# The order of work in the first, the twenty-second and the last tile of a quantized convolution and feed-forward kernel

## The chip, the cores and the metric

The kernel runs on one NeuronCore of one Trainium2 chip. Its engines are TensorE (PE, whose weight loads are listed as PEld), VectorE (DVE), ScalarE (ACT), GpSimd (POOL) and SyncE (SP, which issues nearly all DMAs; its queue is called SPq). They run side by side and wait for one another on semaphores. The metric is the device time of one execution in microseconds (us). Before the change the median of three runs is 294.35 us (294.17 to 295.05).

## The reference

For x of shape (128, 32, 512), the work is a grouped one-dimensional convolution with a per-sample shift, then a feed-forward block in which every activation and every weight is rounded to 8-bit steps of its row, and the residual:

```python
out = conv_general_dilated(x, weight, padding=[(4, 4)], feature_group_count=4)   # 32 -> 32 channels, 9 taps
out = out + ctx[:, :, None] + bias[None, :, None]

def fake_quant(t, axis):
    s = jnp.max(jnp.abs(t), axis=axis, keepdims=True) / 127.0
    s = jnp.maximum(s, 1e-08)
    return jnp.clip(jnp.round(t / s), -128.0, 127.0) * s     # (its value)

def qlinear(x, w):                                            # HIDDEN = 512, INTER = 1376
    return jnp.einsum('bsh,oh->bso', fake_quant(x, -1), fake_quant(w, 1))

h = jax.nn.silu(qlinear(y, w_gate)) * qlinear(y, w_up)        # y = the convolution's output
result = x + qlinear(h, w_down)
```

## The kernel before, in words

The 32 output channels are 32 tiles, numbered 0 to 31. A tile is 128 samples (the partitions) by 512 positions, and it is one row of the feed-forward block for each sample. Its 1376 intermediate columns are cut in three pieces of 512, 512 and 352 columns (`PIECES`, p = 0, 1, 2). The values are kept as whole numbers in bf16, and the scales are multiplied in afterwards.

For one piece p of tile i the work passes through four engines:

1. PE multiplies the quantized row by the gate and the up weights (L1047, `gate_or_up(i, m, p)`, m = 0 for gate and 1 for up). Two PSUM banks serve gate and two serve up, in turn.
2. DVE scales the gate product (L803, `scale_gate`, "gate scaling"), ACT takes silu (L635, `silu`), and POOL multiplies by the row of up scales (L525, `scale_silu`, "silu product").
3. DVE multiplies this by the up product (L813, `multiply_up`), which fills a piece of h_mem and frees the up bank.

When a tile's three pieces are there, DVE takes the row maximum (L819), a scale (L693) and its inverse (L697), together `token_scales(i)`. ACT scales and rounds the row (L640, `round_h`) and turns it into bf16 (L648, `convert_h`). SP transposes it by DMA (L353, `turn_hq`), and PE multiplies it by the down weights four tiles later (L1067, `down(i)`; in the last tile L1117 in two halves, `down_last`). DVE scales that (L831), POOL adds the residual (L533) and SP stores.

The convolution runs in spans (L931 on PE) that are mixed between the tiles. DVE or ACT takes a span out of PSUM (L733, L573), and DVE folds it into maxima (L745). For each group of eight channels DVE makes x_scale and x_inv (L693, L697). ACT then rounds each channel (L580, `round_y`), POOL converts it (L489, `convert_y`), and SP transposes it by DMA (L340, `turn_yq`), since channel n is the input of tile n. The tables `CHANNELS_AT`, `SPANS_AT`, `FOLDS_AT` and others say at which tile an engine does how much of this. Channels 2 and 3 stand at tile 0, channels 24 and 25 (the first of the fourth group) at tile 21, and the fold that completes the fourth group is also at tile 21.

Each engine does its instructions strictly in the order of its own program, and that order is written out by hand in one loop over tiles for each engine. PE's order in tile i is gate p = 0, gate p = 1, up p = 0, then the down product and the spans of the convolution, then gate p = 2, up p = 1 and up p = 2. SP's queue is in order too: a DMA that waits for its source holds back those behind it. In the first tiles it also carries the transposition of the down weights (L334) and, after that, two spans (L312) and four residual loads (L344), then the transposition of channel 6.

The last tile is ordered differently: gate scaling and silu of piece 2 come early there, DVE rounds and converts the first 1024 columns of the last row itself (L883, L887), and the end is finished on DVE (L900, L909, L912).

Of the kernel before, what the change touches and what calls it, by code (L numbers as in the profile page):

```python
# [5 lines left out]
ALU = mybir.AluOpType  # L6
# [21 lines left out]
def adaln_ffn(nc, x, x_windows, cond_ctx_bias, taps_cut, w_gate_up, w_down, out):  # L28
# [19 lines left out]
    SLOTS = GROUPS * SPANS  # L48
# [19 lines left out]
    with ExitStack() as ctx:  # L68
# [3 lines left out]
        def sem(name):  # L72
            return ctx.enter_context(nc.semaphore(name))
# [143 lines left out]
        gate_scaled = sem("gate_scaled")  # L217
        silu_done = sem("silu_done")
        silu_scaled = sem("silu_scaled")
        h_ready = sem("h_ready")  # L220
        h_max_ready = sem("h_max_ready")
        h_scale_ready = sem("h_scale_ready")
# [60 lines left out]
        FOLDS_AT.update({i: [q for q in at if q % 2] for i, at in SPANS_AT.items() if at[0] >= 2 * SPANS + 2 and at[-1] % 2})  # L283
        FOLDS_AT[7] = [2 * SPANS + 1]
        FOLDS_AT.pop(20)
        FOLDS_AT[21] = [SLOTS - 1]

        def down_bank_of(i):
            return conv_bank(i) if TILES - 3 <= i < TILES - 1 else down_bank[i % 2]
# [161 lines left out]
        def _(pool):  # L451
# [81 lines left out]
                pool.tensor_tensor(xo_of(i), xo_of(i), down_out[:, i % 2, :], ALU.add).then_inc(out_ready, 1)  # L533

            for i in range(TILES):
                scale_silu(i, 0)
                if i >= LAG + 1:
                    add_residual(i - LAG - 1)
                scale_silu(i, 1)
                if i == 0:  # L540

                    pool.wait_ge(w_turned, JT)
                    for b in range(HQ_BUFS):
                        pool.memset(hq[b][:, INTER:JT * P], 0.0).then_inc(pad_zero, 1)
                    shift_span(8)
                for o in down_at(i - 1):
                    convert_down(o)
                for n in EARLY_CHANNELS_AT.get(i, []):
                    convert_y(n)
                scale_silu(i, 2)  # L550
                for n in CHANNELS_AT.get(i, []):
                    convert_y(n)
                for q in SHIFTS_AT.get(i, []):
                    shift_span(q)
# [4 lines left out]
        def _(act):  # L559
# [101 lines left out]
                round_down(o)  # L661
            copy_xq(6)
            for i in range(TILES):
                if i:
                    silu(i, 0)
                    silu(i, 1)
                if i == DOWN_ROW_AT + 1:
                    copy_down_row()
                for o in down_at(i - 1) if i else []:
                    round_down(o)  # L670
                if i == TILES - 1:
                    silu(i, 2)
                if i:
                    round_h(i - 1)
                for n in EARLY_CHANNELS_AT.get(i, []):
                    round_y(n)
                if i < TILES - 1:
                    silu(i, 2)
                for n in CHANNELS_AT.get(i, []):
                    round_y(n)  # L680
                for q in SPANS_AT.get(i, []):
                    if q in BY_ACT:
                        copy_span(q)
                if i:
                    convert_h(i - 1)
            round_h(TILES - 1)
            convert_h(TILES - 1)
# [2 lines left out]
        def _(dve):  # L690
# [115 lines left out]
            def multiply_up(i, p):  # L806
                at, n = PIECES[p]
                if i >= H_BUFS:

                    dve.wait_ge(hq_ready, i - H_BUFS + 1)  # L810
                dve.wait_ge(up_done, NP * i + p + 1)
                dve.wait_ge(silu_scaled, NP * i + p + 1)
                dve.scalar_tensor_tensor(h[i % H_BUFS][:, at:at + n], up_bank[(NP * i + p) % 2][:, 0:n], x_scale[:, i:i + 1],  # L813
                                         sg[i % SG_BUFS][:, at:at + n], ALU.mult, ALU.mult).then_inc(h_ready, 1)

# [26 lines left out]
            for i in range(TILES):  # L842
                scale_gate(i, 0)
                if i:
                    multiply_up(i - 1, 2)
                else:
                    weights_top(JT - 1)
                scale_gate(i, 1)
                if i == 0:
                    weights_inverse(JT - 1, 1)  # L850
                if i == TILES - 1:
                    scale_gate(i, 2)
                if i:
                    token_scales(i - 1)
                else:
                    for o in down_at(-1):
                        weights_down(o)
                folds(EARLY_FOLDS_AT.get(i, []))
                if i == 0:
                    for o in down_at(0):  # L860
                        weights_down(o)
                multiply_up(i, 0)
                if i == 0:
                    multiply_up(i, 1)
                if LAG < i < TILES - 1:
                    scale_down(i - LAG)
                if i < TILES - 1:
                    scale_gate(i, 2)
                for q in SPANS_AT.get(i, []):
                    if q in BY_DVE:  # L870
                        add_shift(q)
                if i:
                    multiply_up(i, 1)
                folds(FOLDS_AT.get(i, []))
                if i == LAG:
                    scale_down(0)
                for o in down_at(i) if i else []:
                    weights_down(o)
            def last_quantize():
# [6 lines left out]
                dve.wait_ge(last_h_rounded, 1)  # L886
                dve.tensor_scalar(hq[i % HQ_BUFS][:, 0:LAST_BY_DVE], hi, -MAGIC, 1.0, ALU.add, ALU.mult).then_inc(last_hq_ready, 1)  # L887

            multiply_up(TILES - 1, 2)
            token_scales(TILES - 1)  # L890
            last_quantize()
# [281 lines left out]
```

## Time and profile before

| | us |
|---|---|
| median of three runs | 294.35 |
| the profiled execution | 294.47 |
| its span, first to last instruction | 292.9 |
| PE busy | 281.7 (96%) |
| DVE busy | 251.0 (86%) |
| POOL busy | 202.0 (69%) |
| ACT busy | 194.3 (66%) |
| granted TensorE clock | 1.000 of full speed |

The page's chain of work that ended last is 64% PE, 9% DVE, 9% POOL, 7% DMA and 5% ACT. In a row of the timeline the first number is the start and the second the duration, both in us; a row with "x2" joins two instructions in a run. In square brackets stands how long the engine stood idle before it, and on what: "[1.12 <-DVE h_mem L813]" means that the engine waited 1.12 us and that line 813 on DVE let it go. Neighbouring instructions of one engine overlap in these rows by up to 0.09 us on DVE and ACT, 0.04 us on POOL and 0.16 us on PE.

### The profile page before, as it was taken

The numbers are of one execution on the slowest core, as the hardware profiler recorded it, in microseconds if no ns is written. First come the engines' busy times: TensorE is split into PE (matmuls) and PEld (weight loads), VectorE is DVE, ScalarE is ACT, GpSimd is POOL, SyncE is SP. The second block draws the span as 40 slices with busy tenths as digits, with TensorE's granted clock in tenths as the row PEclk, the third lists the DMA queues.
The fourth block names the chain that finished last, engine by engine and source line by source line (L and its number), as shares of the span: only waits on it lengthen the run. The fifth ranks groups of instructions, "written<-read, shape, count | busy, mean of one in ns | idle before, by whom it ended". The sixth has DMA issues, their size and how long they took to land.

```text
span 292.9 us, 4778 instructions
## 1 busy us (share of the span) xinstructions
PE 281.7 (96%) x1621; PEld 164.4 (56%) x1621; DVE 251.0 (86%) x405; ACT 194.3 (66%) x232; POOL 202.0 (69%) x213
## 2 busy tenths in 40 slices
PE   7998999999999999999999999999989999999995
PEld 7897656655455555554444556665434444444443
DVE  3879879999998988989888878897978889888885
ACT  2258999996686666564888845455688866666640
POOL 1595899998776766663788835556578887666623
PEclk9999999999999999999999999999999999999999
DMA  7999963579846877755489996524256684433355
GB/s 261 416 408 357 410 133 72 113 166 273 214 144 160 203 168 165 208 149 119 128 214 299 239 241 195 166 49 124 73 157 157 159 177 114 87 86 85 100 99 202
DMA packets 83847, 53.36 MB, mean 182 GB/s; under 512 B 69904, under 2 KB 70672, under 8 KB 83696
## 3 DMA queue, kind: packets, MB, share of 16 engines
q1 hardware_dynamic: 83536, 52.89, 67.3%
q10 hardware_dynamic: 288, 0.18, 0.3%
q8 instruction: 13, 0.21, 0.3%
q14 instruction: 10, 0.08, 0.1%
HBM read 27.75 MB, written 8.39 MB: 123 GB/s over the span
## 4 chain that ended last, share of the span: by engine, by line
PE 64%; DVE 9%; POOL 9%; DMA 7%; ACT 5%; issue 4%; SPq 1%; DVEq 0%; POOLq 0%
PE bank L1047 38%; PE bank L1067 19%; PE bank L931 7%; POOL sg_mem L525 4%; DMA xq_mem<-yq_mem 3%; DMA slab<-x_windows 3%; DVE h_mem L813 2%; DVE h_max L819 2%; POOL xq_mem L499 1%; DVE y_part L745 1%; DMA hq_mem<-hq_mem 1%; DVE sg_mem L803 1%; DVE gu_max L704 1%; POOL y_mem L499 1%; ACT sg_mem L635 1%
## 5 line engine op out<-in xcount | busy, mean ns | idle before, releaser
L1047 PE MATMUL bank<-wgu_t,xq_mem 128*128 128x512 bf16 (+1 forms) x768 | 155.9, 357 | 3.1 <-DVE h_mem L813 2.0
L525 POOL TENSOR_TENSOR sg_mem<-sg_mem,gu_scale_row 128x512 f32<-128x512 f32 (+1 forms) x96 | 111.4, 1163 | 64.3 <-ACT sg_mem L635 64.0
L1047 PEld LDWEIGHTS bank<-wgu_t,xq_mem 128*128 128x128 bf16 x768 | 73.7, 98 | 75.2 <-DVE h_mem L813 8.8
L635 ACT ACTIVATE sg_mem<-sg_mem,x_scale 128x512 f32<-128x512 f32 (+1 forms) x96 | 63.7, 674 | 42.5 <-DVE sg_mem L803 42.1
L1067 PE MATMUL bank<-wd_t,hq_mem 128*128 128x512 bf16 (+1 forms) x341 | 78.6, 379 | 0.5 <-DMA hq_mem<-hq_mem 0.5
L813 DVE SCALAR_TENSOR_TENSOR h_mem<-bank,x_scale,sg_mem 128x512 f32<-128x512 f32 (+1 forms) x96 | 66.2, 691 | 10.3 <-POOL sg_mem L525 9.1
L803 DVE TENSOR_TENSOR sg_mem<-bank,gu_scale_row 128x512 f32<-128x512 f32 (+1 forms) x96 | 60.3, 628 | 16.0 <-PE bank L1047 15.6
L640 ACT ACTIVATE h_mem<-h_mem,h_inv 128x1376 f32<-128x1376 f32 (+1 forms) x32 | 45.3, 1414 | 28.1 <-DVE h_inv L697 28.0
L1067 PEld LDWEIGHTS bank<-wd_t,hq_mem 128*128 128x128 bf16 (+1 forms) x341 | 33.3, 98 | 40.9 <-DMA hq_mem<-hq_mem 1.0
L819 DVE TENSOR_REDUCE h_max<-h_mem 128x1 f32<-128x1376 f32 x32 | 50.4, 1576 | 0.0
L931 PE MATMUL bank<-toeplitz_cut,slab 128*128 128x160 f32 (+1 forms) x320 | 44.6, 290 | 1.9 <-DMA slab<-x_windows 1.7
L931 PEld LDWEIGHTS bank<-toeplitz_cut,slab 128*128 128x128 f32 x320 | 43.5, 191 | 4.8 <-DMA slab<-x_windows 2.6
L648 ACT ACTIVATE hq_mem<-h_mem 128x1376 bf16<-128x1376 f32 (+1 forms) x32 | 41.9, 1309 | 0.1
L533 POOL TENSOR_TENSOR xo_mem<-xo_mem,hq_mem 128x512 f32<-128x512 f32 x24 | 30.6, 1273 | 0.0
L831 DVE SCALAR_TENSOR_TENSOR hq_mem<-bank,h_scale,wd_scale_row 128x512 f32<-128x512 f32 x31 | 22.9, 743 | 1.6 <-PE bank L1067 0.8
L580 ACT ACTIVATE y_mem<-y_mem,x_inv 128x512 f32<-128x512 f32 x24 | 16.1, 708 | 2.5 <-DVE x_inv L697 2.5
L745 DVE TENSOR_REDUCE y_part<-y_mem 128x8 f32<-128x1024 f32 x12 | 14.6, 1213 | 1.7 <-POOL y_mem L499 1.7
L489 POOL TENSOR_SCALAR yq_mem<-y_mem 128x512 bf16<-128x512 f32 x22 | 13.3, 619 | 2.2 <-ACT y_mem L580 1.9
L472 POOL TENSOR_SCALAR hq_mem<-hq_mem,gu_inv 128x512 f32<-128x512 f32 (+1 forms) x14 | 9.4, 692 | 6.7 <-DVE gu_inv L717 6.5
L704 DVE TENSOR_REDUCE gu_max<-hq_mem 128x2 f32<-128x1024 f32 (+1 forms) x7 | 8.5, 1210 | 5.3 <-DMA hq_mem<-w_gate_up 5.3
L592 ACT ACTIVATE wgu_t<-bank 128x1024 bf16<-128x1024 int16 (+1 forms) x11 | 10.7, 1001 | 3.1 <-PE bank L947 3.0
L733 DVE TENSOR_TENSOR y_mem<-bank,shift 128x512 f32<-128x512 f32 x17 | 11.3, 681 | 0.6 <-PE bank L931 0.6
(63 smaller groups left out, 138.4 us busy)
## 6 DMA issues: line engine op xcount, KB each, us to landing
slab<-x_windows SPq DMA_DIRECT2D x32, 320.0 KB, 5.4
xo_mem<-x SPq DMA_DIRECT2D x24, 256.0 KB, 3.0
out<-xo_mem SPq DMA_DIRECT2D x24, 256.0 KB, 2.2
hq_mem<-w_gate_up SPq DMA_DIRECT2D x6, 512.0 KB, 6.8
slab<-w_down SPq DMA_DIRECT2D x3, 688.0 KB, 12.5
h_mem<-w_gate_up SPq DMA_DIRECT2D x4, 512.0 KB, 13.6
slab<-x SPq DMA_DIRECT2D x1, 2048.0 KB, 9.3
out<-slab SPq DMA_DIRECT2D x7, 256.0 KB, 2.0
```

The lines of the kernel that those rows point to most:

```text
L525: pool.tensor_tensor(s, s, gu_scale_row[:, 1, at:at + n], ALU.mult).then_inc(silu_scaled, 1)
L533: pool.tensor_tensor(xo_of(i), xo_of(i), down_out[:, i % 2, :], ALU.add).then_inc(out_ready, 1)
L635: act.activation(s, s, ACT.Silu, scale=x_scale[:, i:i + 1]).then_inc(silu_done, 1)
L640: act.activation(hi, hi, ACT.Copy, bias=MAGIC, scale=h_inv[:, i:i + 1]).then_inc(h_rounded, 1)
L648: act.activation(hq[i % HQ_BUFS][:, first:INTER], h[i % H_BUFS][:, first:], ACT.Copy, bias=-MAGIC)\
L803: dve.tensor_tensor(sg[i % SG_BUFS][:, at:at + n], gate_bank[(NP * i + p) % 2][:, 0:n], gu_scale_row[:, 0, at:at + n], ALU.mult).then_inc( ...
L813: dve.scalar_tensor_tensor(h[i % H_BUFS][:, at:at + n], up_bank[(NP * i + p) % 2][:, 0:n], x_scale[:, i:i + 1], sg[i % SG_BUFS][:, at:at + ...
L819: dve.tensor_reduce(h_max[:, one], h[i % H_BUFS], AX_X, ALU.max, apply_absolute_value=True)\
L831: dve.scalar_tensor_tensor(down_out[:, i % 2, :], down_bank_of(i)[:, :], h_scale[:, i:i + 1], wd_scale_row[:, :], ALU.mult, ALU.mult).then ...
L931: last = pe.matmul(out_span[:, :, lo:hi], span_windows(g, i)[:, k, :], toeplitz_cut[:, g, :, tap:tap + hi - lo], start=(k == 0), stop=(k = ...
L1047: last = pe.matmul(bank[n % 2][:, 0:cols], xq_t[:, g, k, P * c:P * (c + 1)], wgu_t[:, m, k, at:at + cols], start=(k == 0), stop=(k == KT - 1))
L1067: last = pe.matmul(down_bank_of(i)[:, :], hq_t[i % HQT_BUFS][0:r, j, :], wd_t[0:r, j, :], start=(j == 0), stop=(j == JT - 1))
```

## The change

Three places are reordered, and one instruction changes its engine. No work is added or dropped.

- **Tile 1.** On ACT, silu of piece 0 goes ahead of the rounding of channels 2 and 3. On POOL, its silu product goes ahead of the conversion of the same channels. On DVE, `multiply_up(1, 0)` goes ahead of `token_scales(0)`.
- **Tile 21.** On ACT, `convert_h(20)` goes ahead of the rounding of channels 24 and 25.
- **Last tile.** On DVE, `token_scales(30)` goes ahead of the third gate scaling. On ACT, `round_h(30)` goes ahead of the third silu. The third silu product moves from POOL to DVE, with a semaphore of its own.

```diff
 pool:
             for i in range(TILES):
-                scale_silu(i, 0)
+                if i != 1:
+                    scale_silu(i, 0)
 ...
-                scale_silu(i, 2)
+                if i < TILES - 1:
+                    scale_silu(i, 2)
+                if i == 0:
+                    scale_silu(1, 0)
                 for n in CHANNELS_AT.get(i, []):
                     convert_y(n)
 act:
             for i in range(TILES):
+                if i > 1:
+                    silu(i, 0)
                 if i:
-                    silu(i, 0)
                     silu(i, 1)
 ...
+                if i:
+                    round_h(i - 1)
                 if i == TILES - 1:
                     silu(i, 2)
-                if i:
-                    round_h(i - 1)
 ...
                 if i < TILES - 1:
                     silu(i, 2)
+                if i == 0:
+                    silu(1, 0)
+                if i == GROUP_3_AT:        # 21
+                    convert_h(i - 1)
                 for n in CHANNELS_AT.get(i, []):
                     round_y(n)
 ...
-                if i:
+                if i and i != GROUP_3_AT:
                     convert_h(i - 1)
 dve:
+                if i == 1:
+                    multiply_up(i, 0)
+                if i:
+                    token_scales(i - 1)
                 if i == TILES - 1:
                     scale_gate(i, 2)
-                if i:
-                    token_scales(i - 1)
 ...
-                multiply_up(i, 0)
+                if i != 1:
+                    multiply_up(i, 0)
 ...
+            def last_scale_silu():
+                at, n = PIECES[NP - 1]
+                s = sg[(TILES - 1) % SG_BUFS][:, at:at + n]
+                dve.wait_ge(silu_done, NP * TILES)
+                dve.tensor_tensor(s, s, gu_scale_row[:, 1, at:at + n], ALU.mult).then_inc(last_silu_scaled, 1)
+
+            last_scale_silu()
             multiply_up(TILES - 1, 2)
```

The order of instructions on DVE at tile 1 before, from the third gate scaling of tile 0 on (bank0 and bank1 are gate banks, bank2 and bank3 up banks):

```order
L803 TENSOR_TENSOR sg_mem<-bank1,gu_scale_row 128x512
L813 SCALAR_TENSOR_TENSOR h_mem<-bank2,x_scale,sg_mem 128x352
L803 TENSOR_TENSOR sg_mem<-bank0,gu_scale_row 128x512
L819 TENSOR_REDUCE h_max<-h_mem 128x1
L693 TENSOR_SCALAR h_scale<-h_max 128x1
L697 RECIPROCAL h_inv<-h_scale 128x1
L813 SCALAR_TENSOR_TENSOR h_mem<-bank3,x_scale,sg_mem 128x512
L803 TENSOR_TENSOR sg_mem<-bank1,gu_scale_row 128x352
```

and now:

```order
L814 TENSOR_TENSOR sg_mem<-bank1,gu_scale_row 128x512
L827 SCALAR_TENSOR_TENSOR h_mem<-bank2,x_scale,sg_mem 128x352
L814 TENSOR_TENSOR sg_mem<-bank0,gu_scale_row 128x512
L827 SCALAR_TENSOR_TENSOR h_mem<-bank3,x_scale,sg_mem 128x512
L833 TENSOR_REDUCE h_max<-h_mem 128x1
L704 TENSOR_SCALAR h_scale<-h_max 128x1
L708 RECIPROCAL h_inv<-h_scale 128x1
L814 TENSOR_TENSOR sg_mem<-bank1,gu_scale_row 128x352
```

The product of tile 1's piece 0 (from bank3) has moved from behind tile 0's row maximum, scale and inverse to ahead of them.

ACT at tile 21 before, from the rounding of row 20 (h_mem) on:

```order
L640 ACTIVATE h_mem<-h_mem,h_inv 128x1376
L635 ACTIVATE sg_mem<-sg_mem,x_scale 128x352
L580 ACTIVATE y_mem<-y_mem,x_inv 128x512 x2
L648 ACTIVATE hq_mem<-h_mem 128x1376
L635 ACTIVATE sg_mem<-sg_mem,x_scale 128x512 x2
```

and now:

```order
L646 ACTIVATE h_mem<-h_mem,h_inv 128x1376
L641 ACTIVATE sg_mem<-sg_mem,x_scale 128x352
L654 ACTIVATE hq_mem<-h_mem 128x1376
L586 ACTIVATE y_mem<-y_mem,x_inv 128x512 x2
L641 ACTIVATE sg_mem<-sg_mem,x_scale 128x512 x2
```

The conversion of row 20 (hq_mem) has moved ahead of the rounding of channels 24 and 25 (y_mem).

DVE in the last tile before, from the second gate scaling on:

```order
L803 TENSOR_TENSOR sg_mem<-bank,gu_scale_row 128x512
L803 TENSOR_TENSOR sg_mem<-bank,gu_scale_row 128x352
L819 TENSOR_REDUCE h_max<-h_mem 128x1
L693 TENSOR_SCALAR h_scale<-h_max 128x1
L697 RECIPROCAL h_inv<-h_scale 128x1
L813 SCALAR_TENSOR_TENSOR h_mem<-bank,x_scale,sg_mem 128x512 x2
L813 SCALAR_TENSOR_TENSOR h_mem<-bank,x_scale,sg_mem 128x352
L819 TENSOR_REDUCE h_max<-h_mem 128x1
```

and now:

```order
L814 TENSOR_TENSOR sg_mem<-bank,gu_scale_row 128x512
L833 TENSOR_REDUCE h_max<-h_mem 128x1
L704 TENSOR_SCALAR h_scale<-h_max 128x1
L708 RECIPROCAL h_inv<-h_scale 128x1
L814 TENSOR_TENSOR sg_mem<-bank,gu_scale_row 128x352
L827 SCALAR_TENSOR_TENSOR h_mem<-bank,x_scale,sg_mem 128x512 x2
L910 TENSOR_TENSOR sg_mem<-sg_mem,gu_scale_row 128x352
L827 SCALAR_TENSOR_TENSOR h_mem<-bank,x_scale,sg_mem 128x352
L833 TENSOR_REDUCE h_max<-h_mem 128x1
```

The third gate scaling has moved behind row 30's maximum, and the silu product of the last piece (L910) is new on DVE.

## Rows read from the trace of the kernel before

**Rows 1.** Page, busy time, share of the span and instructions of PE:

```profile
PE 281.7 (96%) x1621; PEld 164.4 (56%) x1621; DVE 251.0 (86%) x405; ACT 194.3 (66%) x232; POOL 202.0 (69%) x213
```

**Rows 2.** Timeline of PE, whole span (start us, us, line, operation, idle before):

```profile
44.46 3.36 PE L1047 MATMUL bank<-wgu_t,xq_mem 128*128 128x352 bf16 x16 [0.93 <-DVE h_mem L813]
...
75.67 2.76 PE L1047 MATMUL bank<-wgu_t,xq_mem 128*128 128x512 bf16 x12 [0.27 <-DMA xq_mem<-yq_mem]
...
214.96 3.49 PE L1047 MATMUL bank<-wgu_t,xq_mem 128*128 128x352 bf16 x16 [1.12 <-DVE h_mem L813]
...
286.96 2.57 PE L1117 MATMUL bank<-wd_t,hq_mem 128*128 128x256 bf16 x22
```

**Rows 3.** Timeline of tiles 21 and 22, other engines, window 190 to 222:

```profile
209.48 1.33 ACT L580 ACTIVATE y_mem<-y_mem,x_inv 128x512 f32<-128x512 f32 x2 [2.06 <-DVE x_inv L697]
...
210.29 1.23 POOL L489 TENSOR_SCALAR yq_mem<-y_mem 128x512 bf16<-128x512 f32 x2 [1.86 <-ACT y_mem L580]
...
210.72 1.33 ACT L648 ACTIVATE hq_mem<-h_mem 128x1376 bf16<-128x1376 f32 x1
...
211.96 1.32 ACT L635 ACTIVATE sg_mem<-sg_mem,x_scale 128x512 f32<-128x512 f32 x2
...
212.75 1.27 POOL L525 TENSOR_TENSOR sg_mem<-sg_mem,gu_scale_row 128x512 f32<-128x512 f32 x1 [1.24 <-ACT sg_mem L635]
...
214.15 0.75 DVE L813 SCALAR_TENSOR_TENSOR h_mem<-bank,x_scale,sg_mem 128x512 f32<-128x512 f32 x1 [1.17 <-POOL sg_mem L525]
```

**Rows 4.** Timeline of tiles 0 to 2, window 36 to 62:

```profile
39.10 0.69 DVE L803 TENSOR_TENSOR sg_mem<-bank,gu_scale_row 128x512 f32<-128x512 f32 x1 [0.24 <-PE bank L1047]
...
40.54 1.20 POOL L489 TENSOR_SCALAR yq_mem<-y_mem 128x512 bf16<-128x512 f32 x2
...
41.17 0.68 DVE L803 TENSOR_TENSOR sg_mem<-bank,gu_scale_row 128x512 f32<-128x512 f32 x1
...
41.77 1.58 DVE L819 TENSOR_REDUCE h_max<-h_mem 128x1 f32<-128x1376 f32 x1
...
43.65 0.75 DVE L813 SCALAR_TENSOR_TENSOR h_mem<-bank,x_scale,sg_mem 128x512 f32<-128x512 f32 x1
...
43.85 1.43 ACT L640 ACTIVATE h_mem<-h_mem,h_inv 128x1376 f32<-128x1376 f32 x1
...
49.09 0.72 ACT L635 ACTIVATE sg_mem<-sg_mem,x_scale 128x512 f32<-128x512 f32 x1 [0.36 <-DVE sg_mem L803]
```

**Rows 5.** DMA transpositions of inputs, windows 41 to 42 and 227 to 228 (us to landing):

```profile
xq_mem<-yq_mem SPq DMA_TRANSPOSE x1, 3.3
...
xq_mem<-yq_mem SPq DMA_TRANSPOSE x1, 2.4
```

**Rows 6.** Chain that ended last, in order of time (start us, us, what):

```profile
67.89 7.73 DMA xq_mem<-yq_mem
```

**Rows 7.** Timeline of the last tile, window 258 to 293:

```profile
275.81 1.58 DVE L819 TENSOR_REDUCE h_max<-h_mem 128x1 f32<-128x1376 f32 x1
...
277.04 2.15 POOL L525 TENSOR_TENSOR sg_mem<-sg_mem,gu_scale_row 128x512 f32<-128x512 f32 x2
...
277.72 1.46 DVE L813 SCALAR_TENSOR_TENSOR h_mem<-bank,x_scale,sg_mem 128x512 f32<-128x512 f32 x2
277.81 1.44 ACT L640 ACTIVATE h_mem<-h_mem,h_inv 128x1376 f32<-128x1376 f32 x1 [1.29 <-DVE h_inv L697]
...
279.39 0.58 DVE L813 SCALAR_TENSOR_TENSOR h_mem<-bank,x_scale,sg_mem 128x352 f32<-128x352 f32 x1 [0.21 <-PE bank L1047]
...
286.82 2.43 PEld L1117 LDWEIGHTS bank<-wd_t,hq_mem 128*128 128x128 bf16 x22 [0.19 <-DMA hq_mem<-hq_mem]
...
290.09 0.42 DVE L912 TENSOR_TENSOR slab<-slab,sg_mem 128x256 f32<-128x256 f32 x1
```

**Rows 8.** DMA transpositions of rows 30 and 31, windows 280 to 281, 283 to 284:

```profile
hq_mem<-hq_mem SPq DMA_TRANSPOSE x1, 3.9
...
hq_mem<-hq_mem SPq DMA_TRANSPOSE x1, 3.1
```

More of the change, by code:

```diff
@@ L219, in adaln_ffn @@
         silu_scaled = sem("silu_scaled")
+        last_silu_scaled = sem("last_silu_scaled")
         h_ready = sem("h_ready")
@@ L285, in adaln_ffn @@
         FOLDS_AT.pop(20)
-        FOLDS_AT[21] = [SLOTS - 1]
+        GROUP_3_AT = 21
+        FOLDS_AT[GROUP_3_AT] = [SLOTS - 1]
         def down_bank_of(i):
@@ L811, in multiply_up @@
                 dve.wait_ge(up_done, NP * i + p + 1)
-                dve.wait_ge(silu_scaled, NP * i + p + 1)
+                if i == TILES - 1 and p == NP - 1:
+                    dve.wait_ge(last_silu_scaled, 1)
+                else:
+                    dve.wait_ge(silu_scaled, NP * i + p + 1)
                 dve.scalar_tensor_tensor(h[i % H_BUFS][:, at:at + n], up_bank[(NP * i + p) % 2][:, 0:n], x_scale[:, i:i + 1],
@@ L850, in _ @@
                     weights_inverse(JT - 1, 1)
+                if i == 1:
+                    multiply_up(i, 0)
+                if i:
+                    token_scales(i - 1)
                 if i == TILES - 1:
                     scale_gate(i, 2)
-                if i:
-                    token_scales(i - 1)
-                else:
+                if i == 0:
                     for o in down_at(-1):
```

## Prediction

> **What bounds the kernel now.** I read the page first: PE is busy for 281.7 of 292.9 us at full clock [rows 1], so only what stops PE, or what lies behind its last product, can move the time. Then I read PE's timeline for its idle time [rows 2]. The change stands near three of its stops. PE waits 0.93 us at 44.46 for tile 1's first product on DVE, 1.12 us at 214.96 for tile 22's first product, and at 75.67 it waits 0.27 us for the transposed channel 6. The third view is the timeline around each stop, followed backwards from the waiting instruction to the one that let it go. The last is the tail: from 286.82 on PE does the last down product as soon as row 31's transposition has landed, with nothing else left to do [rows 7].
>
> **Tile 21.** At 214.96 PE waits for DVE's L813 at 214.15, that for POOL's silu product at 212.75, and that for ACT's silu at 211.96 [rows 3]. ACT is late for this reason: at 209.48 it comes out of 2.06 us of idling for x_inv of the fourth group, rounds two channels (1.33), converts row 20 (L648 at 210.72, 1.33), and only then takes silu. The change puts the conversion, whose row has long been rounded, into those 2.06 us, where 1.33 fits. Silu then starts at 210.72 instead of 211.96, 1.24 us earlier, provided its gate scaling is there by then (the order before shows silu going straight after the conversion, so this was not its limit). POOL is free at 210.29 + 1.23 = 211.52, just as silu's 0.7 us end, so its product starts near 211.5 instead of 212.75: 1.24 earlier again. DVE idled 1.17 before L813, and with the 0.09 by which its instructions overlap it can start 1.26 earlier at most. PE's stop is 1.12 in matmuls, or up to 1.28 with the 0.16 that neighbouring matmuls otherwise overlap. The smallest of these is 1.24, and the other end is 1.12. I take **-1.24**. Nothing later gives it back: no other matmul row behind it names a wait until the tail, and the transpositions of row 20 and of channels 24 and 25 leave earlier than before.
>
> **Tile 1.** What is late in the wait at 44.46 is DVE's product at 43.65. It stood behind the row maximum (41.77, 1.58) [rows 4]. Now silu starts at 39.10 + 0.69 = 39.79 plus a hand-over, takes 0.72, and ends near 40.55. POOL has just reached this point (40.54), and its product takes 1.27 as in [rows 3], until 41.90. With the 0.13 from POOL to DVE (212.75 + 1.27 = 214.02 to 214.15) the product on DVE starts at 42.03 and ends at 42.78. PE's 0.93 stop is gone. But three things are late in its place.
>
> First, DVE has no idle time here, and its gate scaling at 41.17 ends at 41.85, with the overlap 41.76. The product starts at 42.03, so 0.27 us of idle time is new, and everything behind it on DVE is 0.27 later. The row maximum itself moves from 41.77 to 42.69, +0.92.
>
> Second, ACT's rounding of row 0 at 43.85 waits for this maximum. Its two hand-overs and the inverse stay the same, so it starts at about 44.7, and ACT is +0.87 late from there. At 49.09 ACT had waited 0.36 for DVE, plus 0.09 of overlap. That absorbs 0.45, and the rest, **0.42 to 0.44**, passes on. From there up to the conversion of row 2 I see no ACT row that waits. SP releases its block of DMAs behind that conversion (row 2's transposition, taps, two spans, four residuals), and channel 6's transposition stands last in it. It was issued at 67.89 and took 7.73 us to land [rows 6], and PE starts tile 6 with the landing, at 75.67. PE was there 0.27 earlier. If the block leaves 0.44 later and takes as long, the landing and PE are 0.44 later. PE's own lateness from DVE's 0.27 lies beside this. The bounds are zero, where the block's landing is set by something else and PE's slack of 0.27 takes the rest, and 0.87, where nothing is absorbed at 49.09.
>
> Third, POOL converts channels 2 and 3 behind the new product: from 41.87 instead of 40.54, so channel 2's transposition leaves 1.33 later. It had left at 41.2 and took 3.3 [rows 5], landing at 44.5; PE wants it at 45.06, after the four short matmuls that start at 44.46 (352 columns, 0.6 us). Now it leaves at 42.5. When the queue is quiet such a transposition takes 2.4 [rows 5], and it lands at 44.9 and costs nothing against the old 45.06. With 3.3 it lands at 45.8 and PE is 0.8 to 0.9 late. The 3.3 was taken with a large transposition of down weights still in flight, which by 42.5 has had 1.3 us more, so I take 2.4 and keep 3.3 as a rival.
>
> The 0.93 that PE gains is therefore spent waiting for channel 2, since PE cannot begin tile 2 without it. Tile 1 as a whole is **+0.44**, with bounds 0 and +0.88.
>
> **Last tile.** The row maximum of row 30 no longer stands behind a gate scaling that waits for PE. ACT idled 1.29 before its rounding of row 30 [rows 7], so that rounding can be up to 1.2 earlier. The third silu now stands between it and the conversion and takes at most the 0.72 of a 512-column one. So row 30's transposition leaves some 0.4 to 0.8 earlier and PE does row 30 earlier. None of this is in the sum, because PE then waits for row 31, whose chain gets longer:
>
> - The second product of tile 31 on DVE cannot move: POOL's product for it ends at 277.04 + 1.27 = 278.31, and it started at about 278.4. DVE's two products end at 277.72 + 1.46 = 279.18.
> - Behind it DVE now makes the silu product of 352 columns, both inputs from SBUF. No row has it. The 256-column form is 0.42 [rows 7], the 512-column gate scaling 0.68 [rows 4], so 352 columns is 0.52 in proportion. Until 279.09 + 0.52 = 279.61. Its own result is handed over in about 0.1 (estimate from the 0.13 above; the lower end is 0.03). The last product starts at 279.7 instead of 279.39: +0.32.
> - PE's loads for the last product began at 286.82, released by the DMA, and its matmuls at 286.96, behind row 30's. With row 30 gone early, matmuls start with the loads, and 0.14 comes back. The sum is **+0.18**, with bounds 0 and +0.35.
>
> The Trainium skill ("VectorE: DVE Perf Modes", the errata-adjusted cycle table) gives an fp32 operation between SBUF tiles 58 cycles plus one per column, at 0.96 GHz. By it the new product would take 0.43 (estimate from that page) and this part +0.09. The row of 256 columns says 0.42, where the rule makes it 0.33, so here the trace does not agree with it.
>
> **Sum.** -1.24 + 0.44 + 0.18 = -0.62. The profiled execution's 294.47 (its span of 292.9 and 1.6 around it) becomes 293.85, and taken from the median of 294.35, 0.12 lower, it is **293.7 us**, 0.2% less. A difference of under 0.3% (0.9 us) is what a measurement of this kernel can hardly tell from none, so the likeliest verdict is "no difference".
>
> **The rivals.**
>
> - *A. Tile 1 costs nothing.* The block of DMAs in front of channel 6 lands when it did, because transfers and not ACT's release set it, and PE keeps its time. For it speaks that the landing took 7.73 us against 2.4 in quiet; against it that the block is issued only after ACT's conversion. Sum -1.24 + 0 + 0.1 or so: 293.2 us. Chance 0.24.
> - *B. Channel 2 lands late.* Its transposition keeps 3.3 us. PE is 0.87 late at tile 2, of which nothing is absorbed but a tenth at tile 6. Sum -1.24 + 0.8 + 0.18 = -0.26: 294.1 us. Chance 0.15.
> - *C. Slower: row 31's transposition takes long.* Row 30's took 3.9 us to land and row 31's 3.1 [rows 8]. PE waits for row 31 with nothing else to do. If, at its new issue time, it falls on the long one, the end is 0.8 later, and with +0.44 and +0.18 against -1.24 the sum is +0.18: 294.5 us. It decides from 3.75 us on. With B beside it, it is +0.5. Chance 0.10.
> - *D. Tile 21 does not do what it says.* The wait at 214.96 is replaced by one for another engine on the way: DVE's row maximum of row 21 lies just ahead of the product and ends only 0.1 before its new start. If half of the gain is lost, the sum is 0: 294.35 us. Chance 0.04.
>
> **How the numbers follow.** My forecast (-0.62, its own range 293.3 to 294.1) has 0.47. Faster by over 0.3% means below 293.45: most of A and the lower edge of the forecast, 0.27. Slower by over 0.3% means above 295.25 and needs C with B, or a cost at tile 1 or in the DMA block that I have not seen: 0.06. The rest, 0.67, lies between. The range takes A's 293.2 in, and C's 294.5 on the other side: 293.1 to 294.6.
>
> **What would show it.** Right, if in the profile after:
>
> - ACT's conversion of row 20 stands inside the wait for x_inv, and PE has no stop of over 0.2 us at tile 22 (wrong if another wait of half a us stands there);
> - PE's stop in tile 1 stands one group of matmuls later, with channel 2's transposition as its releaser and tile 2 starting within 0.1 us of 45.06 (B if it is at 45.9);
> - ACT's rounding of row 0 starts near 44.7 and the conversion of row 2 some 0.45 later than before, PE's tile 6 starting near 76.1 (A if at 75.7);
> - the last product's rounding chain is 0.3 later against PE's tile 31, row 30's down product is over before row 31's landing, and PE idles there for 0.5 us or more.
>
> The prediction is wrong as a whole if PE's tile 23 is not 0.7 to 0.9 us earlier than before.

## The result, and the profile after

The changed kernel takes 294.76 us (median of 20 executions, 294.01 to 296.03), the kernel before 293.77 (20 executions): the ratio is 1.0038, interval 1.0029 to 1.0047. It is slower by a hair, where I had forecast 293.7 with a fall of 0.62 and a range up to 294.6. Twelve of its executions stand at 294.0 to 295.0 us (median 294.27) with a mean granted clock of 0.998 or more, eight at 295.7 to 296.0 with 0.992 to 0.994. So the changed kernel is slower at the full clock too, and the low clock comes on top. Of the 126 executions of the kernel before that ran beside the experiments below none showed a clock under 0.998. The profiled execution of after took 294.39 us and is one of the twelve; it lies beside the 294.47 of before, so in these two traces the gains and losses cancel.

PE's timeline, rows with idle time in tile 1 and behind (start us, us, engine, line, operation, [idle before <- releaser]):

```profile
46.47 2.76 PE L1071 MATMUL bank<-wgu_t,xq_mem 128*128 128x512 bf16 x12 [2.42 <-DMA xq_mem<-yq_mem]
...
286.85 2.58 PE L1141 MATMUL bank<-wd_t,hq_mem 128*128 128x256 bf16 x22 [0.95 <-DMA hq_mem<-hq_mem]
```

These are all up to the end. The stops before tile 1's last product, tile 6 and tile 22 [rows 2] are gone. In place of the first stands one of 2.42 us before tile 2, which starts at 46.47 and no longer at 45.06. The chain that ended last names the reason, a transposition that took 3.98 us:

```profile
42.45 3.98 DMA xq_mem<-yq_mem
46.42 0.05 issue
46.47 2.76 PE bank L1071 x12
49.23 2.51 PE bank L955 x20
```

The other engines there and at tile 21 (same columns as the timeline of PE) answer to [rows 3, 4]:

```profile
41.95 0.75 DVE L827 SCALAR_TENSOR_TENSOR h_mem<-bank,x_scale,sg_mem 128x512 f32<-128x512 f32 x1 [0.17 <-POOL sg_mem L527]
42.61 1.58 DVE L833 TENSOR_REDUCE h_max<-h_mem 128x1 f32<-128x1376 f32 x1
```

```profile
44.61 1.44 ACT L646 ACTIVATE h_mem<-h_mem,h_inv 128x1376 f32<-128x1376 f32 x1 [0.48 <-DVE h_inv L708]
...
208.22 1.33 ACT L654 ACTIVATE hq_mem<-h_mem 128x1376 bf16<-128x1376 f32 x1
210.37 1.34 ACT L586 ACTIVATE y_mem<-y_mem,x_inv 128x512 f32<-128x512 f32 x2 [0.82 <-DVE x_inv L708]
211.61 1.32 ACT L641 ACTIVATE sg_mem<-sg_mem,x_scale 128x512 f32<-128x512 f32 x2
```

```profile
278.79 0.52 DVE L910 TENSOR_TENSOR sg_mem<-sg_mem,gu_scale_row 128x352 f32<-128x352 f32 x1
279.43 0.58 DVE L827 SCALAR_TENSOR_TENSOR h_mem<-bank,x_scale,sg_mem 128x352 f32<-128x352 f32 x1
```

The front of the program varies between executions: the last matmul that PE takes for tile 0 starts at 37.7 to 39.1 us in the profiles below. So from here on a moment "+x" counts from that matmul, which starts 0.15 us ahead of tile 1's first gate product. (Where an expectation below puts tile 2 of the kernel before at 7.0 us, it counts from the gate product; that is +7.17 here.) The account of the two profiled executions, PE against before: tile 2 at +8.65 and not +7.17 (+1.48), tile 7 at +47.01 and not +46.07 (+0.94), tile 23 at +177.42 and not +177.68 (-0.26), the landing of the last store at +254.32 and not +254.34. The 2.42 us of the new stop are the 0.93 of the old one, moved to tile 2, and this lateness of 1.48.

### The profile page after: what moved, and what is told of

Same layout as the page of the kernel before. It is cut to its first block, busy times and chain, and to the rows that moved or that the text cites. A ratio compares the mean times of both kernels' runs of the same rounds, so it can differ in the third digit from the quotient of the medians.

```text
span 292.8 us, 4778 instructions
## 1 busy us (share of the span) xinstructions
PE 280.1 (96%) x1621; PEld 163.4 (56%) x1621; DVE 251.8 (86%) x406; ACT 194.6 (66%) x232; POOL 201.2 (69%) x212
## 4 chain that ended last, share of the span: by engine, by line
PE 80%; DVE 7%; DMA 4%; POOL 3%; ACT 2%; issue 1%; SPq 1%; DVEq 0%; POOLq 0%
PE bank L1071 47%; PE bank L1091 24%; PE bank L955 9%; DMA slab<-x_windows 3%; DMA xq_mem<-yq_mem 1%; DVE y_part L756 1%; DVE gu_max L715 1%; ACT wgu_t L598 1%; POOL sg_mem L527 1%; POOL y_mem L501 1%; DVE h_mem L827 1%; SPq L322 1%; POOL slab L535 1%; DVE hq_mem L845 1%; DVE h_max L833 1%
## 5 line engine op out<-in xcount | busy, mean ns | idle before, releaser
L535 POOL TENSOR_TENSOR slab<-slab,hq_mem 128x512 f32<-128x512 f32 x6 | 7.5, 1269 | 6.4 <-DVE hq_mem L845 6.4
```

## The experiments

**One part at a time (e1 to e4).**

```
e1: tile 1's edits alone      e2: convert_h ahead in tile 21 alone
e3: the last tile's edits alone
e4: the changed kernel less tile 1's edits:
-                if i != 1:
-                    scale_silu(i, 0)
+                scale_silu(i, 0)
-                if i == 0:
-                    silu(1, 0)
-                if i == 1:
-                    multiply_up(i, 0)     (and their counterparts put back)
```

> Only the reorder of tile 1. Theory T (channel 2's transposition leaves 1.3 us later, lands later still, PE stands idle for about 2.5 us ahead of tile 2, and in some executions the granted clock falls there): PE's tile 6 is 0.8 to 1.0 us later than before, the fast executions are 0.3 to 1.5 us slower than before, and about half of the executions show a mean clock near 0.994 and 1.8 us more. Rival R (tile 1 is cheap; the loss and the low clock come from the last tile, where PE idles for 1 us ahead of its last product): +0.4 us at most and no execution with a clock under 0.997.

> Only ACT's conversion of row 20 ahead of the rounding of channels 24 and 25. Both theories: PE's stop of 1.1 us at tile 22 is gone, 1.1 to 1.25 us less than before, clock 1.000 in nearly all executions. If it gains under 0.6 us, the gain of tile 21 is given back later even without the rest.

> Only the changes of the last tile. Theory T: row 30's down product 0.7 to 0.9 us earlier, row 31's transposition 0.3 later than without the change, the end 0.1 to 0.3 us later, clock 1.000. Rival R: the idle time of PE ahead of its last product is what lowers the clock, so some executions show 0.994 and 1.8 us more.

> The changed kernel with tile 1 as before (tile 21 and the last tile changed). Theory T: 0.9 to 1.1 us less than before (ratio 0.9965 to 0.997), no execution at a low clock. Rival R: as slow as the changed kernel in half of the executions.

| run | median us (executions) | ratio to before, interval |
|---|---|---|
| e1, tile 1 alone | 297.85 (5) | 1.0121, 1.0097 to 1.0145 |
| e2, tile 21 alone | 293.25 (12) | 0.9964, 0.9948 to 0.9979 |
| e3, last tile alone | 294.73 (11) | 1.0021, 1.0008 to 1.0035 |
| e4, without tile 1 | 292.97 (6) | 0.9964, 0.9950 to 0.9977 |
| before beside them | 294.21 (24) | |

The parts are told apart: tile 21 gains, the last tile costs little (e2 and e4 differ by it and don't differ beyond their intervals), and the whole loss is tile 1's. The medians of e1 and e3 also hold a late front, as far as their profiles tell: tile 0's last matmul starts at 39.1 us in both, at 37.9 in that of before. So 1.0121 is more than tile 1's own cost. In e1 four of five executions had a clock of 0.994. Its profile shows where (window, busy time of the engines, PEclk, DMA share, GB/s), right behind the stop:

```profile
47.74 4.45 PE L1064 MATMUL bank<-wgu_t,xq_mem 128*128 128x512 bf16 x12 [2.46 <-DMA xq_mem<-yq_mem]
```

```profile
48.00:52.00 4.00, 4.00 (x12) 1.53 (x11) 3.07 (x7) 3.17 (x5) 3.58 (x4) 0.57 0.19 44
52.00:56.00 4.00, 3.95 (x29) 3.30 (x30) 2.50 (x5) 2.95 (x4) 2.67 (x3) 1.00 0.76 171
```

The same twelve matmuls take 4.45 us where they take 2.76 in the profile of after: PE ran at 1.2 GHz for most of them, 1.7 us lost.

**Which half of tile 1 costs (e5, e7, e8), and PE kept busy (e6).**

```
e5: the changed kernel, channel 2 ahead of tile 1's silu on ACT and POOL
+                    round_y(n)
+                    if n == 2:
+                        silu(1, 0)         (scale_silu(1, 0) likewise)
e6: e1, and ahead of gate_or_up(2, 0, 0)
+                    for _ in range(32):
+                        pe.matmul(bank[n % 2][:, 0:P], ident_bf, ident_bf)
+                    pe.wait_ge(yq_turned[2], 16)
e7: before, silu(1, 0) and scale_silu(1, 0) moved, multiply_up not
e8: before, multiply_up(1, 0) moved, silu and scale_silu not
```

> The changed kernel, but in tile 0 ScalarE rounds channel 2 and GpSimd converts it before each turns to tile 1's piece 0 (round of channel 2, silu(1,0), round of channel 3; the same order on GpSimd). Theory (what costs in tile 1 is channel 2's transposition, which leaves 1.27 us later and takes 4.0 us): the transposition is issued within 0.1 us of where it was in the kernel before (3.3 us after tile 1's first gate product), PE's stop before up(1,2) shrinks or goes, tile 2's first gate product starts 7.0 us after tile 1's and not 8.65, no wait of over 1 us stands before it, no run shows a granted clock under 0.998, and the time is that of the kernel without tile 1's part, 292.9 to 293.3 us. Rival (tile 1's order costs by what it does on VectorE and ScalarE, whatever channel 2 does): tile 7's first product stays 0.8 us or more later than without tile 1's part, and the time stays at 294 us or above.

> Tile 1's part of the change alone (as e1, 297.9 us), and PE gets 32 matmuls of 128 columns whose result is overwritten, put ahead of tile 2's first gate product, where it waited 2.4 us for channel 2; its wait for the transposition stands behind them. Nothing of the computation is left out. Theory (the low clock of some runs comes from that idle time of PE): tile 2's first gate product starts when it did in e1 (8.7 us after tile 1's), but no stretch at the 1.2 GHz level follows, the granted clock is 0.998 or more in every run, and the time falls by about 2 us, to 295.1 to 295.6 us. Rival (the low clock has another cause, such as what the other engines or the DMA do there): runs at 0.994 remain and the median stays above 297 us.

> The kernel before, with only ScalarE's and GpSimd's half of tile 1's reordering: silu(1,0) and its product ahead of channel 2; VectorE keeps the old order. Theory (channel 2's later departure alone makes the loss): the transposition is issued 1.2 to 1.3 us later and takes 3.9 to 4.0 us, tile 2's first gate product starts 1.4 us or more later than in the kernel before, and the time is 295.1 to 295.6 us with runs at a granted clock of 1.0, about 2 us more with the low clock. Rival (the transposition takes 4 us only together with VectorE's new order, which ends tile 1's products sooner): it takes 3.4 us or less and the time is within 0.5 us of the kernel before's.

> The kernel before, with only VectorE's half of tile 1's reordering: multiply_up(1,0) ahead of token_scales(0); ScalarE and GpSimd keep the old order, so the silu product that it waits for comes as late as before. Theory: channel 2 leaves as before (3.3 us after tile 1's first gate product) and lands within 0.1 us of before, tile 2's first gate product starts within 0.2 us of 7.0; PE's stop before up(1,2) shrinks, but by less than in the changed kernel, as the multiplication now waits on the silu and the row maximum behind it; the time is within 0.4 us of the kernel before's (293.7 us). Rival (VectorE's order by itself delays tile 0's scales and with them channel 2 or the rest of the tiles): tile 7's first product is 0.8 us later or more, and the time 294.5 us or above.

Before beside them took 293.85 (27 executions). e5: 293.75 (ratio 0.9998, 0.9990 to 1.0007). e6: 294.38 (1.0015, 1.0006 to 1.0024). e7: 293.87 (0.9999, 0.9990 to 1.0008). e8: 295.46 (1.0054, 1.0041 to 1.0066). Several of these went against the theory that I had then, "channel 2 leaves late, so it lands late":

- e7 lets channel 2 leave at +4.64, as late as after does, and it took 2.3 us and landed at +6.94, before PE wanted it. The late departure alone costs nothing.
- e6 fell by more than 3 us against e1, where I had expected 2, so not by the low clock alone. Its channel 2 took 2.6 us and tile 2 started at +7.85. As the transposition changed together with PE's idle time, e6 alone proves nothing about the clock.
- e5 did not reach e4's 292.97, although its channel 2 left as early as in before, and e8 lost 1.6 us, as its rival had said. Here VectorE's row says why: the product stands ahead of the row maximum in its queue, and waits for a silu product that is not ready.

```profile
43.14 0.75 DVE L813 SCALAR_TENSOR_TENSOR h_mem<-bank,x_scale,sg_mem 128x512 f32<-128x512 f32 x1 [1.41 <-POOL sg_mem L525]
43.80 1.58 DVE L819 TENSOR_REDUCE h_max<-h_mem 128x1 f32<-128x1376 f32 x1
```

That is e8. In e5 the same wait is 0.65, in after 0.17. DVE has no slack, so its later rows are 1.52 late in e8 and 0.73 in e5, and PE with them. The move pays only if silu is moved as far as the product.

What differs between e7 and after, if channel 2 leaves at the same moment? I looked at the DMA queues in windows of 0.2 us (queue, kind: packets, MB, share). First after, then e7:

```profile
DMA packets 54, 0.03 MB, mean 150 GB/s; under 512 B 53, under 2 KB 53, under 8 KB 53
q8 instruction: 1, 0.02, 36.4%
q1 hardware_dynamic: 53, 0.01, 29.8%
xq_mem<-yq_mem SPq DMA_TRANSPOSE x1, 3.2
```

```profile
DMA packets 68, 0.03 MB, mean 168 GB/s; under 512 B 67, under 2 KB 67, under 8 KB 67
q8 instruction: 1, 0.02, 39.8%
q1 hardware_dynamic: 67, 0.02, 37.7%
```

The first is the window 44.1 to 44.3 of after, near the end of channel 2's data. A single packet of 16 KB on queue 8, an instruction packet, starts there (+6.36) and takes 1.16 us. Channel 2's 512 packets of data have all started by +6.6, as in e9 below. Of the 32 packets of four bytes that close the transfer 30 go at +6.4 to +6.6; the last two go at +7.5, when the big one is over, and the transfer lands at +8.61. The records don't name the DMA engine of a packet; that the big one held the engine of the last two is read from this order. What fills the last 1.1 us they don't show either: in e7 and e9 channel 2 lands 0.3 to 0.4 us after its last closing packet. In e7 the packet starts in 45.4 to 45.6 (+7.71), near the end of channel 3's data. Channel 3 is the one that takes 4.1 us there (two closing packets at +9.0, landing at +10.0), and PE doesn't need it before tile 3. In e5 the packet comes at +6.91, and again it is channel 3 that takes long (3.8 us). The page of after has the whole queue:

```profile
q8 instruction: 13, 0.21, 0.3%
PE 280.1 (96%) x1621; PEld 163.4 (56%) x1621; DVE 251.8 (86%) x406; ACT 194.6 (66%) x232; POOL 201.2 (69%) x212
```

Thirteen packets for 2 x 1621 matmuls and loads is one for every 249 instructions of PE. The Trainium skill ("Advanced Engine Details and Errata", ISA Cache) gives the instruction cache a line of 16 KB, 256 instructions; the packets here have this size and about this distance. In before the first one starts when PE has begun 254 of its instructions and the thirteenth at 3269, 251 apiece on average. So I take them for PE's; the records name no owner. In eight of the ten traces so far the third packet started 0.9 to 1.4 us after PE began tile 1's last product; in the profile of before it came later, at +10.2, and in e6 earlier, at +4.6. The change lets PE begin this product 1.1 us sooner, and the packet starts 1.2 us sooner (+6.36 in after, +7.57 in e4, which differs by tile 1's part alone) and meets channel 2.

**Moving the packet (e9 to e12).** If that is the cause, a few cheap instructions early in PE's program must remove the loss.

```
e9, e10, e11: PE, ahead of conv_span(8), where it waits for its data
+            conv_bank_free(pe, conv_before(8))
+            for _ in range(8):            (e10: 16)
+                pe.matmul(conv_bank(8)[:, 0:8], ident_bf, ident_bf[:, 0:8])
e9, e10 on the changed kernel, e11 on e4
e12: the changed kernel with e6's matmuls, 20 of them
```

> The changed kernel, with 8 matmuls of 8 columns more, whose result is overwritten, put into PE's stop of 1.2 us before the ninth convolution span (15 us ahead of tile 1). They cost nothing there and move every later place in PE's program by 16 instructions. Theory (a 16 KB instruction packet of queue 8 comes when PE reaches a certain place in its program; in the changed kernel that is 6.4 us after tile 1's first gate product, where it holds up one of the 16 DMA engines for 1.16 us in the middle of channel 2's transposition): the packet now comes 8 matmuls earlier, at 4.4 to 4.8 us, ahead of the transposition's data; this takes 2.3 to 2.7 us and not 4.0, tile 2's first gate product starts 7.0 to 7.3 us after tile 1's and not 8.65, no run shows 0.994 or less for the granted clock, and the median is 293.0 to 293.5 us. Rival (the transposition takes 4 us because it leaves late, or because PE waits for it): 8.65 us and 4.0 us stay, and the median stays at 294.0 to 294.8 us.

> As the run with 8 matmuls, but 16 of them, about 1.0 us in a stop of 1.2 us. Theory: the instruction packet comes at 3.2 to 3.8 us, in the last column of w_down's transposition and not in channel 2's; channel 2 takes 2.3 to 2.7 us, tile 2 starts at 7.0 to 7.3 us, and the median is 293.0 to 293.5 us. Rival: as with 8, channel 2 takes 4.0 us and the median stays at 294.0 to 294.8 us.

> The changed kernel without tile 1's part (292.97 us), with the same 8 matmuls. There channel 2 leaves 1.3 us sooner and its data move at about 4.4 to 6.4 us. Theory: the instruction packet comes at 4.4 to 4.8 us and not at 7.6, now into channel 2's transposition, which lands 0.5 to 1.5 us later than at 6.66; tile 2's first gate product is held to that (7.0 us before), and the median rises to 293.3 to 294.5 us: the same 8 matmuls that help the changed kernel cost time here. Rival (the packet doesn't matter, and the 8 matmuls change nothing or the front only): channel 2 lands at 6.5 to 6.8 us, tile 2 starts at 7.0 us, and the median is 292.9 to 293.2 us.

> The changed kernel with 20 matmuls of 128 columns ahead of tile 2's first gate product (1.2 us by the 59 ns that one took in the run with 32), PE's wait for channel 2 behind them. Two causes are told apart, each by its own row. Clock: if PE's idle time of 2.4 us brings the 1.2 GHz stretch, no run shows 0.994 or less, wherever the instruction packet falls, since the idle time is cut to 1.2 us at most; if it is something else in these microseconds, some 4 of 10 runs still show it, as in the changed kernel. Packet: if it falls between 5.5 and 6.5 us after tile 1's first gate product, channel 2 takes 3.5 us or more and tile 2 starts at 8.2 us or later; if it falls elsewhere, 2.3 to 3.0 us, and tile 2 starts at 7.1 to 7.7 us. Time: 294.1 us with the packet inside channel 2's transfer, 293.3 to 293.7 with it outside; 294.8 us or more if the low clock stays.

| run | channel 2 leaves, us to landing | packet starts | tile 2 starts | clock 0.995 or less | median us | ratio to before |
|---|---|---|---|---|---|---|
| after | +4.63, 3.98 | +6.36 | +8.65 | 8 of 20 | 294.76 | 1.0038 |
| e1 | +4.64, 4.01 | +6.41 | +8.69 | 4 of 5 | 297.85 | 1.0121 |
| e7 | +4.64, 2.30 | +7.71 | +7.17 | 0 of 11 | 293.87 | 0.9999 |
| e6 | +4.64, 2.56 | +4.61 | +7.85 | 0 of 11 | 294.38 | 1.0015 |
| e9 | +4.64, 2.47 | +2.17 | +7.15 | 0 of 12 | 293.90 | 0.9986 |
| e10 | +4.64, 2.91 | +2.25 | +7.58 | 0 of 12 | 293.75 | 0.9983 |
| e12 | +4.64, 2.57 | +4.63 | +7.48 | 0 of 12 | 293.55 | 0.9985 |
| e4 | +3.29, 3.37 | +7.57 | +7.17 | 0 of 6 | 292.97 | 0.9964 |
| e11 | +3.84, 3.43 | +2.26 | +7.31 | 0 of 12 | 293.39 | 0.9971 |

PE's row of e9, and its queues over the whole of channel 2's flight (42 to 46 us), with no packet of queue 8:

```profile
45.37 1.90 PE L1074 MATMUL bank<-wgu_t,xq_mem 128*128 128x512 bf16 x8 [0.93 <-DMA xq_mem<-yq_mem]
```

```profile
q1 hardware_dynamic: 1963, 0.49, 72.6%
q14 instruction: 2, 0.02, 1.0%
xq_mem<-yq_mem SPq DMA_TRANSPOSE x2, 2.4
```

With eight small matmuls the changed kernel turns from slower than before (1.0038) to slightly faster (0.9986, interval 0.9973 to 0.9999; e10 and e12 say the same). Two of my numbers failed. The packet moved by more than the instructions that I put in (to +2.2, not +4.6), so how its place follows from the program is not settled. For that reason e11, meant to move the packet into channel 2 there, put it into the transfer ahead: channel 2 landed 0.6 later than in e4, tile 2 started 0.15 later, PE had made that up by tile 7, and the ratio is not to be told from e4's. In e6 and e12 the packet moved too (to +4.6), although their added matmuls come only after that moment in PE's order. The medians of e9 and e10 also stand above my 293.0 to 293.5. Before beside them is at 294.21 too, and I put both down to late fronts, which only the profiled executions show.

So e11 does not give the opposite proof, a packet put into a transposition that was free of it. Other transpositions of the same traces give it. Channel 5 takes 2.4 to 2.6 us in the sixteen traces without such a packet in its flight. In e6 and e12 the next packet of queue 8 starts 1.8 and 2.3 us after channel 5 leaves, and it takes 3.9 and 4.3 us. Channel 3 takes 2.4 to 2.6 us in the thirteen traces without a packet in its flight, and 3.8 and 4.1 in e5 and e7. e12 around channel 5 (59.5 to 64 us), then e9 (59.3 to 62.5 us, no packet of queue 8):

```profile
q8 instruction: 1, 0.02, 1.3%
xq_mem<-yq_mem SPq DMA_TRANSPOSE x1, 4.3
```

```profile
xq_mem<-yq_mem SPq DMA_TRANSPOSE x1, 2.5
```

**The clock, and repetitions (e13 to e16).** In all low-clock executions so far PE had both the 2.4 us of idling and the packet.

```
e13: e9, and PE waits ahead of tile 2 for channel 3 as well
+                    if i == 2:
+                        pe.wait_ge(yq_turned[3 % YQ_BUFS], 16)
e14: the changed kernel again    e15: e1 with e9's 8 matmuls    e16: e4 again
```

> The changed kernel with the 8 small matmuls ahead (e9, where channel 2 lands at 7.1 us and no instruction packet of 16 KB is near), and PE waits before tile 2 for channel 3 too, which lands at 8.3 us. So PE idles for about 2.3 us as in the changed kernel, with no packet in the transfer. If that idle time of PE is what brings the 1.2 GHz stretch, some of these runs (3 in 10 or more) show a granted clock of 0.995 or less, and their times stand 1.5 to 2.5 us above the others'; if the packet or the transfer brings it, none does. Either way tile 2 starts at 8.3 to 8.5 us, and runs at 0.998 or more take 294.0 to 294.5 us (or 1.0 to 1.3 us more where the front starts late).

> The changed kernel itself once more, for a second profile. Theory: a 16 KB instruction packet again starts 6.2 to 6.5 us after tile 1's first gate product, channel 2 takes 3.9 to 4.1 us, tile 2 starts at 8.6 to 8.7 us, and about 4 of 10 runs show 0.992 to 0.994. Rival (the packet's place was one execution's accident): it falls elsewhere, and channel 2 takes under 3 us in this one.

> Tile 1's part alone (e1, 297.9 us) with the 8 small matmuls ahead. Theory: the packet falls ahead of channel 2's data, channel 2 takes 2.3 to 2.9 us, tile 2 starts at 7.1 to 7.6 us, no run at 0.994, and the time is that of the kernel before plus VectorE's and ScalarE's 0.3 to 0.4 us: 294.0 to 294.6 us, over 3 us less than e1. Rival (e1's loss is of another kind): 297 us or more.

> The changed kernel without tile 1's part once more (e4: 292.97 us over 6 runs), to see whether it beats both kernels in another job: 0.8 to 1.2 us under the kernel before, 292.8 to 293.4 us, with the packet at 7.4 to 7.8 us and tile 2 at 7.0 us.

e13: 295.04 us, six of twelve executions at 0.998 or more (293.9 to 294.4 us) and six at 0.992 to 0.994 (295.7 to 296.3). Its profile is one of the six, with the idle time, the clock (PEclk, the value behind POOL's: 0.78 and 0.50) and no packet of queue 8 that starts between 41 and 46.5 us:

```profile
46.16 4.38 PE L1074 MATMUL bank<-wgu_t,xq_mem 128*128 128x512 bf16 x12 [2.20 <-DMA xq_mem<-yq_mem]
```

```profile
44.00:46.00 2.00, 0.00 (x0) 0.00 (x0) 1.93 (x6) 1.52 (x3) 1.46 (x2) 1.00 0.68 87
46.00:48.00 2.00, 1.84 (x7) 0.81 (x8) 1.93 (x5) 2.00 (x4) 1.49 (x3) 0.78 0.01 4
48.00:50.00 2.00, 2.00 (x6) 0.70 (x5) 1.60 (x4) 1.72 (x3) 1.58 (x3) 0.50 0.00 0
```

So PE's idle time brings the low clock without the packet. e14: the packet again at +6.36, channel 2 3.81, tile 2 at +8.48, 296.13 us with seven of twelve executions low (ratio 1.0060, 1.0036 to 1.0083): the collision is not one execution's accident. e15: 294.38 us, 1.0013, none low, against 1.0121 of e1; its channel 2 took 3.1 and tile 2 started at +7.82, both a little more than I had said. e16: 292.98 us, 0.9963, 0.9951 to 0.9976, against 293.90 of before. Its packet started at +8.65, where I had said 7.4 to 7.8 and where the same program had +7.57 in e4. So the packet's moment also varies between executions of one program, as the +10.2 of before had hinted.

The version that beats both kernels is e4, the changed kernel without tile 1's part: 0.9964 and 0.9963 in two jobs.

## Why the prediction was wrong, step by step

**Tile 21: right.** I took -1.24. ACT's conversion stands inside the wait for x_inv, which shrank to 0.82, and PE has no stop at tile 22. From tile 21 to 23 PE takes 15.35 us in before and 14.13 in after (-1.22), 14.12 in e2.

**Last tile: right.** I took +0.18. From the last matmul ahead of tile 31 to the landing of the last store it is 20.47 in before, 20.70 in after, 20.66 in e3. The product without a row took 0.52, which was my value from the 256-column row; the Trainium skill's table ("VectorE: DVE Perf Modes", errata-adjusted) had given 0.43, so the row was the better guide; a note beneath that table says itself that its VectorE row comes out too short. Row 31's transposition took 3.13 again: rival C did not happen.

**Tile 1, DVE: right.** Product at 41.95 (forecast 42.03), row maximum at 42.61 (42.69), 0.17 of new idle time (0.27).

**Tile 1, ACT and channel 6: the chain right, its end wrong, and rival A's mechanism true.** ACT's rounding of row 0 started at 44.61 (44.7), and tile 2's silu on ACT was 0.34 late (0.42 to 0.44). The block of DMAs then left 1.31 late, because PE was late as well. Even so channel 6, issued 1.32 later, landed at 75.62, where it had landed at 75.63: transfers set that landing, not ACT's release. That gave back what PE had waited there [rows 2].

**Tile 1, channel 2: the step that failed.** I wrote that the transposition leaves at 42.5, takes 2.4 "when the queue is quiet" and "lands at 44.9 and costs nothing". It left at 42.45, took 3.98 and landed at 46.42, and PE's tile 2 was 1.48 late: the term that I had put at nothing. Rival B had this step and gave it a chance of 0.15, but with 3.3 us and 0.87. Neither of the two transpositions whose times I weighed (2.4 and 3.3) had such a packet in its flight. The instruction packet is not an issue in the program, and it came 1.2 us sooner with PE's own gain. With the packet away 2.3 to 3.2 us were measured (e7, e9, e10, e12, e13, e15), and tile 1's part costs +0.33 at tile 7 (e9 against e4), near my +0.44. In e9 PE's stop ahead of tile 2 is the 0.93 that I had forecast, and tile 2 starts at +7.15, where before has +7.17. With the packet, tile 2 is 1.5 late and tile 7 1.37 (after against e4).

**The clock: not in the sum at all.** A stop of 2.2 to 2.5 us on PE led to a stretch at 1.2 GHz in 8 of 20, 7 of 12, 4 of 5 and 6 of 12 executions, worth 1.5 to 2.4 us each time, by the medians of the two groups. I had moved PE's 0.93 to tile 2 and gave the length of a single stop no price of its own; with channel 2's lateness on top it became 2.42.

**The base: too high by 0.6, which hides part of the miss.** The median of 294.35 came from three executions; over twenty it is 293.77. The profiled execution of before also waited for channel 6, where that of e7 did not, and its tile 7 is 0.4 later than in e4 and e7. Against 293.77 my sum gives 293.15, and the measured 294.76 is 1.6 above that. That only 1.1 of it shows against the forecast of 293.7 is luck. With the loss removed e9, e10 and e12 come to 0.9983 to 0.9986 of before, 0.4 to 0.5 us less, with intervals that take in my -0.62. So the sum was fair for a kernel whose channel 2 the packet misses.

By its own test (tile 23 earlier by 0.7 to 0.9) the prediction is wrong: it is 0.26 earlier. The whole is 1.37 lost at tile 1, of it 0.43 that the profile of before had already lost on channel 6, 1.22 gained, 0.23 lost at the end; and in two executions of five the clock on top. Losses and gains cancel in these two profiles; over all executions at the full clock the changed kernel is 0.5 us slower (294.27 against 293.77).

## What to carry to other kernels

When a change takes away a stop on PE, what hangs on PE's place in its program can come sooner, here an instruction packet by 1.2 us; look in the DMA queues, not only in the issues, for what else is in flight around a transfer that has little slack. Price the longest single stop of PE apart from the sum of its stops, since behind 2.2 to 2.5 us of idling the clock was at half in many executions. Moving a consumer forward in an in-order queue needs its producer moved as far, or the consumer's wait is charged to everything behind it (e8: 1.41 us of waiting, 1.6 us of time).

## What was not expected of the hardware

- One 16 KB instruction packet of 1.16 us made a transposition of 2.3 to 3.2 us take 3.8 to 4.0; two of its 32 closing packets went only when the big one was over. It does so in whichever transposition it meets near the end of the data: channel 2 in after, channel 3 in e5 and e7 (3.8 and 4.1 us), channel 5 in e6 and e12 (3.9 and 4.3).
- Eight matmuls of 8 columns, 16 us ahead of tile 1, changed the time by 0.5%: the ratio went from 1.0038 to 0.9986. What fixes the packet's place is open: 8 and 16 of them moved it to +2.17 and +2.25, and matmuls behind it to +4.6.
- Low clock follows idle time on PE by chance: at 2.2 to 2.5 us of idling 25 of 49 executions showed it, where PE waited 1.6 us or less there (e2 to e12, e15, e16) none of 133.
